# A four-layer graph network on one core: the load reordered, products of X in banks of their own, and one more chunk combined by GpSimd

## The reference

```
L0: deg = max(rowsum(adj) + 1, 1);  h = (adj @ x + x) / deg
    y = relu([x, h] @ W + b);       out = y / max(norm(y), 1e-12)
L1: h = tanh([x, t] @ W1 + b1);     xb = x @ B.T
    out = h @ W2 + b2 + adj @ xb - rowsum(adj) * xb
L2: rank = cumsum(adj != 0, axis=1); deg = rank[:, -1]; k = min(deg, 100)
    w = mask * where(rank - (deg - k) > 0, 0.5 ** (k - pos), 0); out = w @ (x @ weight) + bias
L3: exponential map of x, adj @ that, logarithmic map, @ kernel + bias
```

## Time and profile before

| | us |
|---|---|
| median of 3 runs | 166.24 (165.58 to 166.6) |
| the profiled execution's own time | 165.22 |
| its span | 163.3 |
| PE busy | 112.1 (69%) |
| DVE busy | 101.6 (62%) |
| ACT busy | 70.2 (43%) |
| POOL busy | 55.8 (34%) |
| mean granted clock of TensorE | 0.921 |

### The profile page before, as it was taken

One profiled execution on the slowest core, in us unless ns is written; L12 is line 12 of the kernel. 1 busy time (PEld: TensorE's weight loads), 2 busy tenths in 40 slices (PEclk: granted clock), 3 DMA queues, 4 the chain that ended last, 5 costly groups with the idle time before them and its releaser, 6 DMA issues.

```text
span 163.3 us, 3084 instructions
## 1 busy us (share of the span) xinstructions
PE 112.1 (69%) x1228; PEld 64.5 (40%) x1244; DVE 101.6 (62%) x227; ACT 70.2 (43%) x119; POOL 55.8 (34%) x67
## 2 busy tenths in 40 slices
PE   0000277658799559999679699999989899992000
PEld 0000156657124313546333366595446644561000
DVE  0064993999853999993969313545303888538861
ACT  0030213603749668954589745141034310257440
POOL 0000040132920936652145303416203461723290
PEclk9999999985559999999999999999999999999555
DMA  3999999999999992000000000000000000000006
GB/s 78 259 290 260 357 303 305 343 345 300 303 342 342 254 283 66 0 4 2 0 4 0 0 4 0 0 4 0 0 4 0 0 0 2 0 4 0 0 0 129
DMA packets 13950, 18.73 MB, mean 115 GB/s; under 512 B 5360, under 2 KB 5488, under 8 KB 13936
## 3 DMA queue, kind: packets, MB, share of 16 engines
q1 hardware_dynamic: 7728, 9.74, 21.5%
q10 hardware_dynamic: 6208, 8.78, 19.0%
HBM read 18.00 MB, written 0.52 MB: 113 GB/s over the span
## 4 chain that ended last, share of the span: by engine, by line
PE 43%; DVE 28%; DMA 7%; issue 6%; POOL 5%; ACT 4%; ACTq 2%; POOLq 1%; DVEq 0%
PE psC L892 7%; DMA stage<-adj 7%; PE psN L892 7%; PE psS L892 7%; DVE AT L612 6%; DVE AT L613 6%; PE psS L944 3%; POOL root L325 3%; PE psC L926 3%; PE psH L936 2%; POOL nroot L344 2%; PE psC L979 2%; PE psH L1033 2%; PE psH L1034 2%; DVE X L697 1%
## 5 line engine op out<-in xcount | busy, mean ns | idle before, releaser
L445 ACT ACTIVATE WT<-psC 128x1024 int16<-128x1024 f32 x32 | 31.1, 1024 | 10.8 <-PE psC L984 10.7
L325 POOL TENSOR_TENSOR root<-var,power 128x4 f32<-128x4 f32 (+1 forms) x16 | 18.7, 1173 | 44.2 <-DVE var L692 18.3
L936 PE MATMUL psH<-AT,cb 128*32 128x256 bf16 (+3 forms) x96 | 5.9, 374 | 20.8 <-DVE AT L613 20.7
L892 PE MATMUL psS<-AT,XP 128*128 128x512 bf16 x72 | 19.0, 386 | 1.0 <-issue 0.6
L612 DVE STREAM_TRANSPOSE AT<-stage 128x1024 bf16<-128x1024 bf16 x10 | 13.2, 1316 | 10.2 <-DMA stage<-adj 10.2
L892 PE MATMUL psN<-AT,XP 128*128 128x512 bf16 x44 | 11.1, 379 | 3.9 <-DVE XP L618 3.6
L613 DVE STREAM_TRANSPOSE AT<-stage 128x1024 bf16<-128x1024 bf16 x10 | 12.8, 1278 | 0.0
L338 POOL TENSOR_TENSOR XB<-X,weights 128x256 f32<-128x256 f32 x12 | 10.0, 849 | 5.6 <-DVE X L697 5.6
L936 PEld LDWEIGHTS psH<-AT,cb 128*32 128x32 bf16 x96 | 2.3, 106 | 24.1 <-issue 20.7
L892 PEld LDWEIGHTS psS<-AT,XP 128*128 128x128 f16 x80 | 7.3, 99 | 10.5 <-issue 3.8
L979 PE MATMUL psC<-later,cb 32*32 32x512 bf16 x256 | 9.8, 426 | 1.6 <-ACT WT L445 1.1
(11 more groups left out here) (162 smaller groups left out, 226.4 us busy)
## 6 DMA issues: line engine op xcount, KB each, us to landing
stage<-adj SPq DMA_DIRECT2D x20, 256.0 KB, 14.7
stage<-adj ACTq DMA_DIRECT2D x20, 256.0 KB, 10.5
WT<-adj ACTq DMA_DIRECT2D x12, 256.0 KB, 12.8
WT<-adj SPq DMA_DIRECT2D x12, 256.0 KB, 16.2
out<-X SPq DMA_DIRECT2D x6, 64.0 KB, 1.9
weights<-weights_packed SPq DMA_DIRECT2D x1, 353.5 KB, 17.6
cb<-constants_packed SPq DMA_DIRECT2D x1, 264.2 KB, 11.7
X<-x SPq DMA_DIRECT2D x2, 128.0 KB, 7.3
```

Of the source, the lines that this page charges most:

```text
L325: nc.gpsimd.tensor_tensor(root[:, e, 0:n], var[:, e, 0:n], power[:, 0:n, 0:NR], ALU.pow).then_inc(root_ready, 1)
L445: nc.scalar.activation(WT[:, e, tiles], psC[:, PAIRS * h:PAIRS * (h + 1)], ACT.Relu).then_inc(chain_taken, 1)
L892: ins = nc.tensor.matmul(sum_bank(l, e), XP[:, l % 2, c], matrix, start=(c == 0), stop=last)
L936: ins = nc.tensor.matmul(psH[QD * g:QD * (g + 1), cols], one, AT[:, NQ * g + k, e, cols], start=(k == 0), stop=(k == NR - 1))
```

## The change

The order of the load is changed on both queues, so that pieces 0 and 1 go ahead of x. The constants go to ACT's queue, behind x. On DVE, piece 1 is turned ahead of the maximum of x, the means of x come right after that maximum, piece 2 is turned ahead of the low part, `take_degrees(0)` is ahead of piece 5, and `take_degrees(1)` behind piece 10 and `split1(0)`. The products of x use `psN` and `psS` in turn. Degrees of chunks 1 to 3 have the bank `psX`, no longer `psH`. `chain(0)` and `chain(1)` are ahead of most of the products of x, and ACT takes them there. The combination of chunk 2 goes to POOL, with a new semaphore `yc_ready`. POOL takes `var_root(0, 2)` and `diagonals(3)` ahead of `l2_root(3)`, and waits for the last split before `residual(1, 2)`. `centre("W2", "K")` is ahead of `take_degrees(3)` on DVE.

```diff
         def z_bank(e):
-            return (psN[:], psC[:, 1], psC[:, 2], psC[:, 3])[e]
+            return (psN[:], psS[:])[e % 2]
+
+        def deg_bank(e):
+            return psH if e == 0 else psX
...
             load_lower(0)
+            load_lower(1)
             for q in range(NQ // 2):
                 sp.dma_start(X[QD * q:QD * (q + 1)], xd[q]).then_inc(x_loaded, 16)
-            load_lower(1)
-            sp.dma_start(cb[:].bitcast(U16), cpack).then_inc(consts_loaded, 16)
+            load_lower(2)
             sp.dma_start(weights[:, 0:first], wpack[:, 0:first]).then_inc(own_weights_loaded, 16)
-            for m in range(2, NR):
-                load_lower(m)
+            load_lower(3)
...
                 pool.wait_ge(ssroot_ready, e + 1)
+                if e == 2:
+                    pool.wait_ge(yc_ready, 1)
...
             l2_root(2)
+            combine(2)
             weigh(3)
+            var_root(0, 2)
+            diagonals(3)
             l2_root(3)
-            var_root(0, 2)
             var_root(0, 3)
-            diagonals(3)
+            pool.wait_ge(parts_ready, parts_count(1, 3))
             residual(1, 2)
...
             load_upper(0)
+            load_upper(1)
             for q in range(NQ // 2, NQ):
                 act.dma_start(X[QD * q:QD * (q + 1)], xd[q]).then_inc(x_loaded, 16)
-            for m in range(1, 6):
+            act.dma_start(cb[:].bitcast(U16), cpack).then_inc(consts_loaded, 16)
+            for m in range(2, 6):
                 load_upper(m)
...
             take_z(0)
+            take_step(0)
+            load_upper(9)
             take_xt(0, 2)
-            load_upper(9)
             take_z(1)
+            load_upper(10)
+            take_step(1)
             take_xt(0, 3)
-            load_upper(10)
+            load_upper(11)
             take_z(2)
             take_z(3)
-            load_upper(11)
-            take_step(0)
+            take_counts(1)
             load_upper(12)
-            take_step(1)
-            take_counts(1)
+            take_step(2)
             load_upper(13)
-            take_step(2)
             take_spread(1)
...
             transposes(0)
+            transposes(1)
             dve.wait_ge(x_loaded, 16 * NQ)
             nc.vector.tensor_reduce(xs[:, 0:1], X[:].rearrange("p c f -> p (c f)"), AX_X, ALU.max,
                                     apply_absolute_value=True).then_inc(xmax_ready, 1)
-            transposes(1)
+            step(nc.vector.tensor_reduce(xmean[:], X[:], AX_X, ALU.add))
+            nc.vector.tensor_scalar(xmean[:], xmean[:], -1.0 / D, None, ALU.mult).then_inc(xmean_ready, 1)
             dve.wait_ge(xmax_all, 1)
...
-            step(nc.vector.tensor_reduce(xmean[:], X[:], AX_X, ALU.add))
-            nc.vector.tensor_scalar(xmean[:], xmean[:], -1.0 / D, None, ALU.mult).then_inc(xmean_ready, 1)
+            transposes(2)
             dve.wait_ge(high_ready, 1)
...
-            for m in range(2, 5):
-                transposes(m)
+            transposes(3)
+            transposes(4)
+            take_degrees(0)
+            transposes(5)
...
-            transposes(5)
-            take_degrees(0)
             transposes(6)
...
-            take_degrees(1)
             variance0(0)
             transposes(10)
             split1(0)
+            take_degrees(1)
             add_own_part(1)
...
             activate0(2)
+            centre("W2", "K")
             take_degrees(3)
-            combine0(2)
+            variance0(2)
             add_own_part(3)
             activate0(3)
             normalise(0, 2)
             combine0(3)
-            centre("W2", "K")
             normalise(0, 3)
...
                     if l == 0 and e >= 1:
                         pe.wait_ge(sum_taken, e)
+                        pe.wait_ge(z_taken, NE)
...
+                if l == 1 and e < 2:
+                    pe.wait_ge(deg_taken, NE - 1 + e)
...
                 pe.wait_ge(xt_taken, e + 1)
+                if e % 2 == 1:
+                    pe.wait_ge(sum_taken, 1)
+                if e >= 2:
+                    pe.wait_ge(z_taken, e - 1)
...
             def degrees(e):
-                pe.wait_ge(spread_taken, e + 1)
+                pe.wait_ge(spread_taken, 1) if e == 0 else pe.wait_ge(counts_taken, e + 1)
+                if e >= 2:
+                    pe.wait_ge(deg_taken, e)
+                if e == NE - 1:
+                    pe.wait_ge(hid_taken, 1)
...
                 e, m = i // NR, i % NR
-                if i == 0:
-                    pe.wait_ge(z_taken, NE)
...
                 if l == 0:
-                    pe.wait_ge(deg_taken, e + 1)
+                    pe.wait_ge(spread_taken, e + 1)
                     if e == 0:
+                        pe.wait_ge(deg_taken, 1)
...
             degrees(0)
+            chain(0)
             transpose_x(0, 2)
             own_part(1)
             dense(0, 0)
+            chain(1)
             transpose_x(0, 3)
             own_part(2)
             own_part(3)
-            chain(0)
-            chain(1)
...
                     if c == 5:
                         spread(e)
-                    if c == 9:
+                        degrees(e)
+                    if c == 11:
                         chain(NR * e - 1)
-                        degrees(e)
...
-            transpose_x(1, 1)
+            degrees(e)
             spread(e)
             sums(1, 0, range(1, 2))
-            degrees(e)
             chain(10)
             dense(0, e)
+            transpose_x(1, 1)
             hidden(1)
```

More of the change, by code:

```diff
@@ L138, in gnn_kernel @@
         y_ready = sem("y_ready")
+        yc_ready = sem("yc_ready")
         ysq_ready = sem("ysq_ready")
@@ L623, in take_degrees @@
                 dve.wait_ge(deg_ready, e + 1)
-                step(nc.vector.tensor_scalar(degp[:, cs], psH[:, cs], 1.0, 1.0, ALU.add, ALU.max))
+                step(nc.vector.tensor_scalar(degp[:, cs], deg_bank(e)[:, cs], 1.0, 1.0, ALU.add, ALU.max))
                 step(nc.vector.scalar_tensor_tensor(floor[:, cs], degp[:, cs], 1e-24, degp[:, cs], ALU.mult, ALU.mult))
-                nc.vector.tensor_scalar(ndeg[:, cs], psH[:, cs], -1.0, None, ALU.mult).then_inc(deg_taken, 1)
+                nc.vector.tensor_scalar(ndeg[:, cs], deg_bank(e)[:, cs], -1.0, None, ALU.mult).then_inc(deg_taken, 1)
             def add_own_part(e):
@@ L672, in activate0 @@
                 step(nc.vector.tensor_reduce(ymean[:, chunk(e)], ye, AX_X, ALU.add))
-                step(nc.vector.scalar_tensor_tensor(ye, per_node(ymean[:, chunk(e)]), -1.0 / D, ye, ALU.mult, ALU.add))
+                ins = nc.vector.scalar_tensor_tensor(ye, per_node(ymean[:, chunk(e)]), -1.0 / D, ye, ALU.mult, ALU.add)
+                if e == 2:
+                    ins.then_inc(yc_ready, 1)
+                else:
+                    step(ins)
             def combine0(e):
@@ L958, in degrees @@
             def degrees(e):
-                pe.wait_ge(spread_taken, e + 1)
+                pe.wait_ge(spread_taken, 1) if e == 0 else pe.wait_ge(counts_taken, e + 1)
[3 more added lines that the diff above has]
+                    pe.wait_ge(hid_taken, 1)
                 for r in range(NR):
                     c = NR * e + r
-                    ins = nc.tensor.matmul(psH[:, c:c + 1], cnt[:, r].rearrange("p Q b -> p (Q b)"),
+                    ins = nc.tensor.matmul(deg_bank(e)[:, c:c + 1], cnt[:, r].rearrange("p Q b -> p (Q b)"),
                                            C("each"), start=True, stop=True)
@@ L1086, in _ @@
                 if e == 1:
+                    chain(NR * e + 1)
                     sums(1, 0, range(0, 1))
-                    chain(NR * e + 1)
                 if e == 2:
```

## The result

| | before | after |
|---|---|---|
| median, us (runs) | 166.36 (4) | 161.34 (161.34, 161.86, 159.61, 161.33) |
| ratio after to before | | 0.9709, 95% interval 0.9621 to 0.9798 |
| profiled execution, us | 165.22 | 161.34 |
| its span, us | 163.3 | 159.5 |
| mean granted clock | 0.921 | 0.930 |

The change makes the kernel 2.9% faster. 162.3 us was forecast, 160.0 to 165.9 as the range. The runs of after differ by 2.3 us among themselves, and go with their clock: the one of 159.61 us had a mean of 0.945, the others 0.930 to 0.932. What follows has to be read with that in mind.

A forecast was written before the change was run, and what follows sets the result against it. No single engine bounds the load: late transfers, PE's 3.38 us gap with low clock and DVE's 4.28 us wait do; then PE. 2.9 + 1.0 = 3.9 us off the profiled 165.22 gives 161.3, median 162.3, range 160.0 to 165.9.

The forecast's parts named there:

- The removed wait of 4.28 us: DVE's wait for chunk 1's degrees goes, 1.2 us handed back to late pieces: counts of chunk 2 2.9 us earlier.
- Pieces 6 to 9: Load: constants on ACT's queue delay pieces 6 and 7 by 1.6 us, to 36.3 and 39.3; piece 9 ends at 48.5.
- my own lower bound: Load, pieces 6 and 7: a delay of 0 instead of 1.6 us, if SP's lighter queue gives way.
- The reading that ACT's queue and not DVE sets both pieces: Load before: DVE starts pieces 6 and 7 at 34.71 and 37.75, as their transfers land at 34.7 and 37.7.
- the rival of pieces as early as before: Load: constants don't delay ACT's pieces, piece 11 ends 1.3 us earlier than in the sum; 161.0 us, chance 0.16.
- Its other half: Same rival, PE in the load: the clock doesn't fall, because PE isn't idle for 3.38 us; chance 0.16.
- The start: Start of the load on DVE: x last in at 15.8 us, f16 parts of x at 22.6, 1.3 us later.
- The low clock moves on: Rival, PE: the clock falls around chunk 2's counts after a 3.2 us wait, costing 6.1 us; 168.4 us, chance 0.12.
- The condition that I gave: Slower rival, PE ahead of chunk 2's counts: the fall decides from a gap of about 3.4 us on.
- The end of layer 0: Last split of chunk 3: PE's wait of 1.31 us mostly goes, worth 1.0 us (bounds 0.7 and 1.5).
- The pair of rows by which I doubted that GpSimd is the slower engine: End of layer 0: POOL 0.73 us against DVE 0.72 for the same sum, against the skill's 2 times slower.
- The 1.0 us that I added from profile to median: Whole kernel: the median was 1.0 us above its profile, so 161.3 profiled became 162.3 us.

The follow-up runs named there:

- e2: The changed kernel with chain(0) and chain(1) moved back behind own_part(3) on PE and ACT's list there as before: 159.01 us, ratio 0.9579.
- e7: The kernel before with one edit, take_degrees(0) ahead of piece 5 on DVE: 162.47 us against 165.01, ratio 0.9893.
- e8: The kernel before with 14 matmuls of unread results added ahead of dense(0, 0), nothing released earlier: 162.73 us, ratio 0.9851.
- e11: The changed kernel with chains 0 and 1 late and take_degrees(0) behind piece 5, both undone together: 161.06 us, ratio 0.979.
- e5: The changed kernel with take_degrees(0) behind piece 5 and the bias products again: 160.0 us, ratio 0.9683.
- e3: The changed kernel with the end of layer 0 undone on DVE and POOL, chunk 2 combined by DVE: 159.38 us, ratio 0.9595.
- after_again: The changed kernel, unedited, run once more in a later set on the same chip: 160.12 us, ratio 0.9685.
- e12: The changed kernel with load order, chains and end of layer 0 undone; the degrees' places and bank and the x-product banks kept: 160.5 us, ratio 0.9723.
- e6: The changed kernel with the handling of chunk 1's and 2's degrees on PE and DVE undone: 161.93 us, ratio 0.9853.
- e4: The changed kernel with overwritten matmuls added ahead of own_part(3) and the counts of chunks 1 and 2: 158.67 us, ratio 0.9577.
- e10: The changed kernel with chains 0 and 1 late and matmuls added ahead of the counts of chunks 1 and 2: 160.52 us, ratio 0.9732.

## Why the prediction was right, and where it was right by luck

The time (162.3 against 161.34) and the sign came out. Point by point:

- **The removed wait of 4.28 us is the mechanism, as forecast.** It is gone in after, and it is what the lead at the counts of chunk 2 consists of. But its cause was only half told. I put it down to PE's late and slow work ahead of chunk 1, and in the change to the chains moved into the gap. e2 shows no worth of the chains' place, and e7 shows that the earlier taking of chunk 0's degrees alone brings the wait to 0.85 us in the kernel before. e8 brings it to 1.86 us with nothing released earlier, by a low clock that comes later and ends sooner. So the gap of 3.38 us and the clock behind it account for most of the wait. Three things were seen to close the gap or fill it, all but 0.4 to 0.5 us of it: the degrees' earlier taking (e7), the later f16 parts with the earlier piece 4 (e11), and added matmuls (e8). That the first two overlap follows from e5 and e11, in which it stays closed. The chains ahead stand in it too, but no run has them without one of the others.
- **Pieces 6 to 9, sized wrong.** I put 1.6 us for the constants on ACT's queue. Pieces 6 and 7 were turned 0.2 and 0.3 us later, not 1.6. The profile after, the issues that answer to the earlier trace rows:

```profile
L406 ACTq DMA_DIRECT2D WT<-adj x4: 332/452/453, 23.7 to 25.0; - x4
...
DMA to landing us min/median/max: 9.2/10.6/13.0
```

  Issued 1.6 us later, they land sooner after that: those of piece 6 by 33.7 us, where it was 34.7, those of piece 7 by 38.0, where it was 37.7. I had taken the queue's rate (1.5 us for 256 KB) for proof that it was full from its start. Either it still had slack, or SP's transfers gave way, which was my own lower bound: SP's of piece 8 land at 37.6 and 38.7 us, before at 36.5 and 37.7. No run tells the two apart. The reading that ACT's queue and not DVE sets both pieces was too strong as well. In before DVE came free at 34.58 and 37.83, within 0.15 us of the landings, and in after piece 6 had been in for 1.2 us when DVE got to it. This made counts of chunk 1 come at 40.59 instead of 41.8, and those of chunk 2 at 55.61 instead of 56.7: 4.0 us of lead instead of 2.9. In this part the rival of pieces as early as before (0.16, 161.0 us) came true, and its time is nearer to the 161.34 than mine. Its other half, a clock that doesn't fall, did not.
- **The start** was about right in its result (f16 parts at 22.96 for 22.6, degrees of chunk 0 waited for 1.66 for 1.5 us), by another way: x was in at 14.4, not 15.8, and piece 2 was late (19.34). The reduction over partitions was covered by the means.
- **The low clock moves on: the rival did happen, in small.** I gave it 0.12 and the price of a stretch of 12.2 us. It came at the named place, the counts of chunk 2, behind a wait of 1.70 us and not of 3.4, and lasted some 3 us. It took most of the 1.6 us by which the lead shrinks (2.4 at the last counts of chunk 3): from the counts of chunk 2 to there after takes 16.35 us, the kernels that have the new list of PE and no fall there 15.04 or 15.05, and before 14.76. The condition that I gave, a gap of 3.4 us, was wrong: the gap of the earlier trace rows was only the longest one, not the least that does it. And the length of the gap before it doesn't decide alone: e3 waits 1.66 us at the same place and its counts take 1.05 us.
- **The end of layer 0, 1.0 us: right in size (1.45 in the profile), wrong in cause.** Of the stretch from the last counts of chunk 3 to the dense part of layer 1 (20.49 before, 19.04 after) 0.76 us go to PE's list, with the degrees ahead of the spread. The rest goes with the wait of 1.31 us, which e3 shortens to 0.50 with this end as before on DVE and POOL. The stretch is 20.48 and 20.49 us in e7 and e8, which have the old list of PE, and 19.03 in e3, which has the new one. Neither GpSimd's combination nor the other changes there moved the time (e3). The pair of rows by which I doubted that GpSimd is the slower engine (0.73 against 0.72) was badly chosen: DVE's 0.72 ran beside a product on POOL, and the same sum took DVE 0.42 us at 85.88, against 0.73 for GpSimd.
- So 3.9 us were forecast and 3.88 measured in the profile, as 2.9 + 1.0 against 4.0 - 1.6 + 1.45. The agreement to a tenth is luck. The 1.0 us that I added from profile to median wasn't there: median and profile are both 161.34. And the median hangs on how many runs had the second fall, three of four here; in after_again it is 160.12.

**What the parts are worth.** Against the kernel before: chunk 0's degrees taken earlier 1.1% (e7). All of the degrees with PE's new list and the banks for products of x 2.8% (e12). All of the change 2.9 to 3.15%. By e6 the handling of chunk 1's degrees would have 1.7% (0.9853 over 0.9685), but that comes with a clock that fell more often in e6's few runs. The load's order, the chains ahead and GpSimd's combination together can't be told from nothing, and the intervals leave room for about 1%.

**Open:** whether e6's edit brings more falls of the clock, or its few runs happened to have them. Which part of e12 the banks for the products of x have, for they weren't tried alone. And whether filling every gap, as in e4, beats the changed kernel, which wants runs of both side by side.

## What to carry to other kernels

When an engine has a gap in front of a stretch that turns out slow, fill the gap with work that nobody reads before any reordering: that one run tells the clock from the order, and here it was about half of the whole gain (1.5 of 2.9%). Put the added work where the clock is still up: behind a gap left open it runs slowly itself and holds up what follows (e10). When several edits are made at once, undo them one at a time and also start from the old kernel with one of them, for edits that close the same gap each look worthless when undone alone. And when the runs of one program differ by more than the effect that is sought, set the clock of each run beside its time before calling a difference an effect.

## What the runs showed of the hardware

The granted clock fell behind waits of PE much shorter than the 3.38 us of before: behind 1.36 us in e10, behind 1.70 us in after (1.90 us for counts that take 1.05), and behind the wait of 1.24 us for ACT ahead of hidden(1) in after_again and not in after, with the same program. It stayed up behind others as long: 1.67 and 1.50 us in before, at 56.69 and 59.60. The runs of after, after_again and e5 differ by 2.3 to 2.7 us accordingly, and with the gaps filled (e4) by 1.1. The Trainium skill (TensorE: Matmul & The Clock Gate, Why this matters for your kernels) warns of gaps between bursts of matmuls. These runs agree in kind (3.38 us in before), and show shorter ones to matter (1.24 to 1.70 us).

The reduction over partitions on POOL, row of 0.38 us, whose cover I had feared for, takes at most some 1.3 us with its signals: in after the maximum ends at 15.62 us, and DVE went from the means to the scales (16.87 us) without a wait. GpSimd's products of two 128x256 f32 tiles took 0.61 to 0.62 us and its sum of two 0.73, where DVE's rows without POOL beside them say 0.42 for either.
